# A fused gated block on one core: attention in five parts inside the feed-forward loop, a new order of the front, and fewer filler products

## What is computed

```python
x = x + tanh(g_xattn[0]) * wkv(w, u, k=layernorm(x), v=ctx)          # recurrence over the 64 tokens
g, up = split(layernorm(x) @ ternary(w_gate_up).T)                     # 256 -> 2 x 1024
x = x + tanh(g_ffn[0]) * (rms_norm(silu(g) * up) @ ternary(w_proj).T)  # 1024 -> 256
s = where(mask, layernorm(x) @ ctx.T / sqrt(256), -1e30)               # 64 x 64 per sequence
x = x + tanh(g_xattn[1]) * (softmax(s) @ ctx)
q = layernorm(x); scale = max(abs(q)) / 448                            # one maximum over all tokens
x = x + tanh(g_ffn[1]) * (float8(q / scale) @ w_lin.T + bias)
```

## Time and profile before

| | us |
|---|---|
| median of the 3 runs | 163.47 |
| lowest, highest | 163.19, 165.22 |
| the profiled execution, device time | 165.08 |
| its span, first to last instruction | 163.3 |
| busy: PE, DVE, ACT, POOL | 129.8, 111.1, 90.4, 34.7 |
| mean granted TensorE clock, as a share of full speed | 0.912 |

### The profile page before, as it was taken

The page is one execution under the profiler, slowest core; times in us unless marked ns, Lnnn a source line. Parts: engine busy times, 40 slices in busy tenths (PEclk is TensorE's granted clock), DMA queues, the critical chain, the costliest instruction groups (busy, mean ns, idle before and its releaser), DMA issues. The chain is left out here.

```text
span 163.3 us, 2227 instructions
## 1 busy us (share of the span) xinstructions
PE 129.8 (79%) x769; PEld 85.4 (52%) x769; DVE 111.1 (68%) x256; ACT 90.4 (55%) x165; POOL 34.7 (21%) x70
## 2 busy tenths in 40 slices
PE   6748999969998999908948999999637876990970
PEld 6537984324333657605525666766435744860760
DVE  5957997779999899545882566124546699926930
ACT  3542698044857868893447777584762316327121
POOL 7712000049000000000764002300361032300600
PEclk9955799987999999995799999999987999999598
DMA  4899800000000000000000000000000000000033
GB/s 139 273 362 366 253 9 2 0 0 0 0 0 4 2 0 0 0 0 4 0 0 0 2 0 4 2 0 0 4 0 0 0 0 0 4 0 2 0 128 130
DMA packets 7094, 6.90 MB, mean 42 GB/s; under 512 B 1320, under 2 KB 6826, under 8 KB 7082
## 3 DMA queue, kind: packets, MB, share of 16 engines
q1 hardware_dynamic: 7072, 6.75, 12.7%
q10 hardware_dynamic: 10, 0.00, 0.0%
HBM read 5.70 MB, written 1.05 MB: 41 GB/s over the span
## 5 line engine op out<-in xcount | busy, mean ns | idle before, releaser
L832 PE MATMUL ps<-wT,xhi 128*128 128x512 bf16 x64 | 25.3, 395 | 0.7 <-ACT xlo L542 0.7
L833 PE MATMUL ps<-wT,xlo 128*128 128x512 bf16 x64 | 25.3, 395 | 0.0
L1215 DVE SCALAR_TENSOR_TENSOR hbuf<-ps,pscale,sil 128x512 f32<-128x512 f32 x16 | 11.9, 747 | 15.7 <-PE ps L833 7.8
L406 POOL TENSOR_SCALAR ve<-mv 128x2 f32<-128x2 f32 (+2 forms) x11 | 2.4, 215 | 72.2 <-DVE mv L1097 72.0
L891 PE MATMUL ps<-wT,wgu_raw 128*128 128x256 bf16 x128 | 17.5, 282 | 0.0
L1091 DVE BATCH_NORM_STATS2 stats<-xs 128x6 f32<-128x256 f32 x32 | 12.4, 413 | 3.1 <-DMA xs<-in_x_dram 2.7
L570 ACT ACTIVATE sil<-ps 128x512 f32<-128x512 f32 x16 | 9.6, 598 | 8.3 <-PE ps L833 8.2
L583 ACT ACTIVATE wgu_raw<-ps 128x512 f16<-128x512 f32 x16 | 9.6, 597 | 8.1 <-PE ps L871 8.1
L891 PEld LDWEIGHTS ps<-wT,wgu_raw 128*128 128x128 f16 x128 | 13.0, 101 | 1.6
L1103 DVE TENSOR_SCALAR xn<-xs,mv,rstd 128x256 f32<-128x256 f32 x26 | 11.7, 498 | 1.3 <-POOL rstd L395 0.9
L531 ACT ACTIVATE wscale<-ps 128x1024 bf16<-128x1024 f32 x6 | 6.1, 1025 | 9.3 <-PE ps L754 9.3
(11 more groups left out here) (165 smaller groups left out, 277.4 us busy)
## 6 DMA issues: line engine op xcount, KB each, us to landing
wgu_raw<-in_L_ffn_w_gate_up_dram SPq DMA_DIRECT2D x4, 512.0 KB, 8.8
ctx_sb<-in_ctx_dram SPq DMA_DIRECT2D x2, 512.0 KB, 8.3
wp_raw<-in_L_ffn_w_proj_dram SPq DMA_DIRECT2D x1, 1024.0 KB, 10.4
out_dram<-xs SPq DMA_DIRECT2D x4, 256.0 KB, 2.2
xs<-in_x_dram SPq DMA_DIRECT2D x2, 256.0 KB, 2.9
xs<-in_x_dram SPq DMA_DIRECT2D x1, 512.0 KB, 7.6
wlin_raw<-in_L_ffn_weight_dram SPq DMA_DIRECT2D x1, 256.0 KB, 9.2
bias_bc<-in_L_ffn_bias_dram SPq DMA_DIRECT2D x1, 128.0 KB, 8.8
```

The source lines that it names most:

```text
L832: pe.matmul(ps[:, bank, :], xhi[:, h, c, o:o + P], w, start=(c == 0), stop=False)
L833: mm = pe.matmul(ps[:, bank, :], xlo[:, h, c, o:o + P], w, start=False, stop=(c == CH - 1))
L1215: dve.scalar_tensor_tensor(out=hbuf[:, b, :], in0=ps[:, 1 + b, :], scalar=pscale[:, 0:1], in1=sil[:, b, :], op0=ALU.mult, op1=ALU.mult).th ...
```

## The change

Attention now has five parts of 2, 2, 2, 1 and 1 tiles, with one PSUM bank each. Parts 0 and 1 go through their softmax inside the feed-forward loop: transposes and scores in units 9 to 11, the exponentials in ScalarE's unit 12 between two added table loads, the attention products behind unit 14. Parts 2 to 4 follow behind the loop, interleaved on VectorE, with `project(15)` ahead of them on TensorE. `y_back(1)` stands ahead of `h_left(5)`, and `h_high(5)` and `h_high(12)` stand ahead of the silu behind them. GpSimd's four `weight_part` steps stand behind the work for parts 0 and 1. In the front VectorE normalises x's first half before it waits for the second half of x, and runs `wkv(0)` before it normalises the second; `front_keys(1)` stands behind weight transposes 2 and 3. Of the 38 filler products, 12 are left: 6 ahead of `weight_sums` and 6 near the end. Only the last transposes and the amax of part 4 stand between those 6 and the turning of the maximum, and `residual_back(3)` stands behind it.

The diff, cut to its core:

```diff
-WARM_FFN = 8
-WARM_LAST = 10
+WARM_LAST = 6
...
-    PARTS = [(0, 4), (4, 2), (6, 1), (7, 1)]
-    SPACE = [(6, 7), (4,), (5,), (0,)]
+    PARTS = [(0, 2), (2, 2), (4, 2), (6, 1), (7, 1)]
+    EXP_UNIT = 12
+    SPACE = [6, 7, 4, 5, 0]
...
-    WARM_FRONT = 10
+    WARM_FRONT = 6
...
             power(1, 6, 2, 3)
+            mean_square(0)
+            power(2, 0, 2, 1)
+            mean_square(1)
+            power(2, 2, 2, 2)
             for n in range(4):
...
             for n in range(UNITS):
+                if n in (6, EXP_UNIT + 1):
+                    h_high(n - 1)
                 silu(n)
...
-                if n == 13:
+                if n == 10:
                     channels_in(qT, 0, qT_ps, qT_ready)
+                if n == 11:
+                    channels_in(qT, 1, qT_ps, qT_ready)
+                if n == EXP_UNIT:
+                    act.preload_act_table_set("natural_log_exp_and_others")
+                    softmax_exp(0)
+                    softmax_exp(1)
+                    act.preload_act_table_set("silu_and_others")
+                if n == EXP_UNIT + 2:
+                    attn_in(0)
+                    attn_in(1)
...
             weight_rest(1)
             spread_scales()
-            keep_warm(WARM_FRONT, 0, wabs)
             ffn_in(0)
...
             weight_rest(2)
-            pe.wait_ge(G_ready, CHUNKS * CH)
-            keep_warm(WARM_FFN, 0, wabs)
             for n in range(UNITS + 2):
...
                 if n >= 2:
                     project(n - 2)
+                if n == 6:
+                    y_back(1)
...
-                if n == 12:
+                if n == 9:
                     channel_major(2, 0, qT_ps)
-                if n == 14:
+                if n == 10:
+                    channel_major(2, 1, qT_ps)
                     scores(0)
-                if n == 16:
-                    channel_major(2, 1, qT_ps)
-
-            probs_back(0)
-            scores(1)
+                if n == 11:
+                    scores(1)
+                if n == EXP_UNIT + 1:
+                    probs_back(0)
+                    probs_back(1)
+                if n == EXP_UNIT + 2:
+                    attend(0)
+                    attend(1)
...
+            ln_apply(0, 0, TPC, 1)
             dve.wait_ge(in_x[2], 16)
             ln_stats(0, TPC, TPC)
-            ln_apply(0, 0, TPC, 1)
+            wkv(0)
             ln_apply(0, TPC, TPC, 2)
-            wkv(0)
```

More of the change, by code:

```diff
@@ L592, in channels_in @@
                 first, n = PARTS[q]
[L593 to L598 removed]
+                act.wait_ge(ps_sem, q + 1)
+                act.activation(out[:, :, first * P:(first + n) * P],
+                               ps[:, SPACE[q], 0:CH * n * P].rearrange("p (c t) -> p c t", c=CH), ACT.Copy).then_inc(done, 1)
             def softmax_exp(q):
@@ L616, in _ @@
                     square(n - 1)
-                    h_high(n - 1)
+                    if n not in (6, EXP_UNIT + 1):
+                        h_high(n - 1)
                     h_low(n - 1)
@@ L899, in scores @@
                 first, n = PARTS[q]
-                pe.wait_ge(qT_ready, sum(len(SPACE[r]) for r in range(q + 1)))
+                pe.wait_ge(qT_ready, q + 1)
                 for i in range(n):
@@ L914, in probs_back @@
                 for i in range(n):
-                    t = pe.transpose(ps[:, SPACE[q][-1], i * P:(i + 1) * P], E[:, first + i, :], ident[:, :])
+                    t = pe.transpose(ps[:, SPACE[q], i * P:(i + 1) * P], E[:, first + i, :], ident[:, :])
                 t.then_inc(ET_ps, 1)
@@ L978, in _ @@
             front_values(1)
+            weight_transposes(2)
+            weight_transposes(3)
             front_keys(1)
-            for p in range(2, PAIRS):
-                weight_transposes(p)
+            weight_transposes(4)
+            weight_transposes(5)
             pe.wait_ge(neg_ready, 2)
```

172 lines of the change are left out of this document (87 added, 85 removed).

## The result

| | kernel before | changed kernel |
|---|---|---|
| median (lowest to highest) | 163.83 us (163.19 to 165.22, 4 runs) | 157.80 us (155.29 to 160.90, 4 runs) |
| ratio, 95% interval | | 0.9477 [0.9367, 0.9587] |
| profiled execution, its span | 165.08, 163.3 | 155.57, 153.8 |

The ratio, a gain of about 5%, compares only the executions of the faster state, 155.29 and 155.57; the two others took 160.03 and 160.90 at a lower granted clock, 0.935 and 0.923 against 0.967.

The account below looks back on a forecast made before the run. No engine was full; a row of stages with different limits bounds the kernel. Gains 5.3 + 4.6 - 7.7 + 6.6 + 2.8 - 0.6 = 11.0 us, off the 163.47 median, gave 152.5 us, range 149.0 to 157.5.

Parts of the forecast that it names:

- front, at the table load: Start to the exchange's table load: earlier normalisation and keys plus fewer fillers gain 5.3 us, bounds 2.5 to 5.6.
- exchange to unit 8: Table load to gate(8): y_back(1) fills the wait and normalisations escape GpSimd contention; gain 4.6 us, bounds 3.0 to 5.2.
- units 8 to 15: Feed-forward loop from gate(8) to the last gating product: added attention work loses 7.7 us, bounds 5.5 to 11.
- tail: Last gating product to the maximum: less VectorE work and idling, 22.9 instead of 29.5 us, gain 6.6.
- turning: Maximum to its turning: fillers now run ahead of part 4's transposes, 2.87 shrinks to 0.05 us, gain 2.8.
- clock: TensorE's half clock across the kernel: waits in five places and fewer fillers cost 0.6 us, between 0 and 2.8.
- 4 of 10 are gone: Front: fillers had held weight sums beyond the last weight copy; with fewer, scales come at 26.2, gaining 3.8 us.
- Rival A: Loop waits bring the clock down, once in units 10 to 14 and once in the tail: 155.5 us, chance 0.14.
- B: Front gains only 2.5 us because weights arrive late or the second half's keys wait: 155.3 us, chance 0.11.
- C: Slower than before: TensorE stays at 1.2 GHz from unit 10 through unit 15, 169.5 us, chance 0.02.
- D: Loop waits cost less, ScalarE running ahead: loop loses 5.5 us, clock nothing, 149.7 us, chance 0.06.
- E: Unit 12's two table loads cost the skill page's 5.3 us, standing 2.7 longer: 155.2 us, chance 0.01.

Follow-up runs that it names:

- old_front: Changed kernel with the front's old order on VectorE, TensorE and ScalarE, smaller filler counts kept: median 162.18 us, against 159.54 for the changed kernel on that chip.
- b_exchange: Kernel before with only y_back(1) ahead of h_left(5), h_high(5) ahead of silu(6) and a second squares buffer: median 161.20 us against 164.53.
- b_turn: Kernel before with 6 fillers, not 10, ahead of the last part's transposes, residual_back(3) left ahead of them: median 163.35 us, ratio 0.9944.
- b_front: Kernel before with only the front's new order and fewer fillers: median 161.47 us against 164.53, ratio 0.9845.
- fill_back: Changed kernel with the front's 22 removed filler products put back: median 159.41 us, against 159.54 for the changed kernel on that chip.
- no_exchange: Changed kernel without unit 12's two table loads, a same-shape copy replacing the exponentials of parts 0 and 1 (output wrong): median 153.90 us.
- later_steps: Changed kernel with TensorE's steps of parts 0 and 1, and VectorE's softmax_in(1), placed later: median 151.37 us, ratio to the kernel before 0.9222.
- old_turn: Changed kernel with 10 fillers back between the last part's transposes and the turning of the maximum: median 161.93 us.
- fill_waits: Changed kernel with filler products in three TensorE waits: behind the scales, ahead of y_back(1), and ahead of h_left(12): median 155.61 us.

## Why the prediction was right, and where it was not

The profiled executions differ by 9.5 us; the forecast was 11.0. It was then set against the median of 163.47, 1.6 below the profile that it was laid out on; these two, 1.5 and 1.6, are why the faster executions lie 3.1 above 152.5. The terms, from the table:

| term | predicted | measured | from |
|---|---|---|---|
| front, at the table load | +5.3 | +4.8 | 67.34 to 62.58 |
| exchange to unit 8 | +4.6 | +4.1 | 17.67 to 13.59 |
| units 8 to 15 | -7.7 | -8.8 | 28.83 to 37.59 |
| tail | +6.6 | +6.2 | 30.07 to 23.91 |
| turning | +2.8 | +2.7 | 3.03 to 0.30 |
| behind the turning | 0 | +0.5 | 16.4 to 15.8 |
| clock | -0.6 | in the terms above | |

*Front.* The mechanism was right (recurrence at 12.11, scales 3.2 earlier), and `old_front` shows the order worth about 2.3. That the stage came out at 4.8, so near the 5.3, is in part luck. Three profiles have the old front: before and `b_exchange` reach the table load at 67.34 and 67.74, `b_turn` at 64.40, and against this one the stage is worth 1.8. All profiles of the new front with few fillers lie from 61.66 to 64.22, and `b_front` gains 3.1 by the medians; that is the better figure, and the term was too large by about 2. The prediction also took the old durations of the front as fixed, while the clock was at half there from 8.0 to 18.5. The step on the fillers ("4 of 10 are gone", and 8 ahead of the loop for 1.7) failed in part: `fill_back` puts all 22 of the front back, and the table load comes 0.3 later than in an execution whose clock is down, 1.4 later than in one whose clock recovers. Filler products were priced as time in a list; with them the clock was also back sooner.

*Exchange.* By the medians the order of `y_back(1)` and `h_high(5)` is worth 3.3 (`b_exchange`), most of the 4.1. By stage, 1.5 of it shows at an equal length of half clock; the rest goes with a shorter fall and quicker normalisations, which `b_front` had without the order.

*Units 8 to 15.* ScalarE's silu of each unit against 3.25 us gives the extra time of each: unit 8 1.6 (forecast 1.6), unit 9 1.1 (0.45), unit 10 2.45 (2.3), unit 11 2.0 (1.9), units 12 and 13 together 2.8 (2.7), unit 14 3.0 (2.95). Only unit 9 was missed: its transposes wait 0.39 for a normalisation and push the unit. That is most of the 1.1 by which the term was too small. `no_exchange` shows 2.36 of it to be the two loads, `later_steps` shows another 5.4 (6.2, less 0.9 that moved into the tail) to come of where the steps stand, 3.2 of them the three waits.

*Tail.* 19.0 us of VectorE's work against 18.9, and 4.5 idle against 4.0.

*Turning.* The gain was forecast and came, and `old_turn` shows it to hang on the fillers' place. The prediction counted `residual_back(3)` only as work that fits into a later wait; in `b_turn`, where it stands ahead, it is what the fillers come behind.

*Clock.* This is the term that was mis-sized: "I add 0.6, between 0 and 2.8". In three of eight executions there was no such loss: the mean clock was above that of the profile before (0.966 and 0.967 against 0.912), and the 0.5 behind the turning is the clock's. In five the clock fell again, in unit 13 behind the wait of 2.18 and in the last stage, and cost 4.0 by the two profiles (1.0 in the front less 0.4 at the exchange, 1.7 in units 8 to 15, 1.7 behind the turning). Rival A named the place and took 3; set on a base of 155, it gives about 158, and the measured 159.5 to 161.3 are beyond the range's upper end of 157.5. The argument against it, that the waits are at most half as long as the 4.44, did not hold: behind 2.17 the clock fell, behind 2.18 in another execution it did not. That the wait is the cause is likely and not shown to the end: with fillers in it (`fill_waits`), with 1.41 (`later_steps`) and with none (`no_exchange`) unit 13 ran at full clock, in one profile each.

*The other rivals.* B showed as five waits of 0.35 to 0.41, with the scales 0.6 late in one profile and 0.1 in the other. C did not occur; after each fall the clock came back within 4 us in units 8 to 15. D is excluded for the changed kernel, whose loop lost 8.8. E, the page's price, is excluded: the loads at 100.34 and 102.95 take 1.28 each. The Trainium skill ("ScalarE: Activation LUTs", section "Table sets: the hidden batching unit") gives some 2.7 for each; by this trace and by `no_exchange`, 2.36 for both together, that is too much. The prediction set against it the section of the same page of the Trainium skill on what a load costs; but that section has 2.66 in all, about 1283 ns for the load and the rest for a drain. The load agrees with these traces, and beside it the rows leave no room for a drain: the exponentials start at 101.63, where the first load ends. The advice to batch by set still points the right way, since the pair stands on the path.

## What to carry to other kernels

Steps inserted in a loop should find their operands ready: try each a unit later than the first in which it could run, and read each wait of the limiting engine in order of time. Moving five steps of TensorE, most by one unit, took 5.4 us off the way from gate(8) to the maximum here, where leaving out the table loads took 2.4. Before reading a gain by stage, take a second profile of the kernel before: here the same front differed by 2.9 between two profiles. And price a filler product at both levels of the clock before cutting it: where a kernel's runs fall in two groups, compare the granted clock by stage in a profile of each before looking for a cause in the data flow.

## What the runs showed of the hardware

- The same wait of TensorE (2.18 and 2.17 us ahead of `h_left(12)`) was followed by half clock in one execution of the changed kernel and not in another; in `later_steps`, where it is 1.41, unit 13 ran at full clock.
- In the four kernels with the front's old order (before, `b_exchange`, `b_turn`, `old_front`) TensorE's clock was at half for 3.5 to 10.5 us between 8.0 and 19.5, and in none of the ten with the new one ahead of 30.0, in one profile each. With the old order TensorE waits 2.49 to 4.13 us for the first normalised tiles.
- The clock can fall while TensorE is fully busy: 4.00 of 4.00 us from 106.5 to 110.5. The idle time lies ahead of the fall, and the cost is paid by work that has nothing to do with it.
- VectorE's normalisation of a tile took 0.87 beside GpSimd's weight steps (1.73 for two at 87.95, GpSimd busy from 87.69) and 0.35 without (1.38 for four at 7.94). With both in the same lists, four took 3.76 in one profile and 2.59 in another: in the first they started 0.2 behind GpSimd's first weight step (80.65 and 80.46), in `b_front` 0.5 ahead of it (76.85 and 77.38).
